# Cross-attention probabilities turned by VectorE and DMA in place of TensorE, the division moved behind the weighting

## What is computed

```python
q_big = einsum('bshk,hkq->bshq', (x @ Wq.T).reshape(8, 56, 16, 128), w_kc_q)   # 16 heads
kv_r = rope(kv_c)                                  # context, 8 x 1500 x 64
q_r = einsum('bshq,hqr->bhsr', rope(q_big), W_qr)  # layer 3: no rope on q
k_r = einsum('bld,hdr->bhlr', kv_r, W_kr)
scores = einsum('bhsr,bhlr->bhsl', q_r, k_r)
attn = softmax(scores, axis=-1)                    # over the 1500 context rows
ctx_c = einsum('bhsl,bld->bhsd', attn, kv_r)       # the weighted context
out = einsum('bhsd,hkd->bhsk', ctx_c, w_kc_kv) @ Wo.T
```

## Time and profile before

| | |
|---|---|
| time, median of 3 runs | 1666.74 us (1664.62 to 1668.67) |
| profiled execution, its span | 1666.3 us |
| PE busy | 1627.4 us, 98% |
| PEld busy | 1104.8 us, 66% |
| DVE busy | 1113.9 us, 67% |
| ACT busy | 749.9 us, 45% |
| POOL busy | 239.1 us, 14% |
| DMA | 71.10 MB, mean 43 GB/s |

### The profile page before, as it was taken

How to read it: one execution, slowest core, us unless ns; L and a number is a source line. 1 busy time by engine, 2 the same in 40 slices (tenths; PEclk the granted TensorE clock), 3 DMA queues, 4 the chain that set the end, 5 groups by cost and what they waited for, 6 DMA issues and landing times.

```text
span 1666.3 us, 35653 instructions
## 1 busy us (share of the span) xinstructions
PE 1627.4 (98%) x15234; PEld 1104.8 (66%) x15234; DVE 1113.9 (67%) x1974; ACT 749.9 (45%) x1297; POOL 239.1 (14%) x428
## 2 busy tenths in 40 slices
PE   9999999999999899999999999999999999999998
PEld 5575367777755666655377777764566767777765
DVE  3735899999566763266899999435445289999623
ACT  2223366666413641144366666312444366666411
POOL 0011300000010313011200000010455000000030
PEclk9999999999999999999999999999999999999999
DMA  8302020000040011051020000050300220000010
GB/s 280 86 13 83 1 78 2 2 2 2 2 187 1 2 59 40 1 133 48 1 97 2 2 2 2 4 240 0 64 1 1 114 89 2 2 2 2 2 44 11
DMA packets 35522, 71.10 MB, mean 43 GB/s; under 512 B 25359, under 2 KB 29775, under 8 KB 31433
## 3 DMA queue, kind: packets, MB, share of 16 engines
q1 hardware_dynamic: 35240, 68.71, 12.6%
q10 hardware_dynamic: 126, 0.11, 0.0%
HBM read 68.36 MB, written 0.46 MB: 41 GB/s over the span
## 4 chain that ended last, share of the span: by engine, by line
PE 89%; DVE 6%; ACT 2%; POOL 1%; issue 1%; DMA 1%; SPq 0%; DVEq 0%; POOLq 0%; ACTq 0%
PE ps L1122 14%; PE ps L1135 14%; PE ps L1035 13%; PE ps L1501 9%; PE ps L361 9%; PE ps L946 3%; PE ps L2599 3%; PE ps L1150 3%; PE ps L528 2%; PE ps L1961 2%; PE ps L956 1%; POOL arena L1795 1%; PE ps L2626 1%; PE ps L982 1%; PE ps L967 1%
## 5 line engine op out<-in xcount | busy, mean ns | idle before, releaser
L1236 ACT ACTIVATE arena<-ps,softmax_stats 128x1500 f32<-128x1500 f32 x168 | 253.8, 1511 | 193.0 <-DVE softmax_stats L1317 190.8
L1135 PEld LDWEIGHTS ps<-arena,ctx_pos 125*64 125x64 f32 x4608 | 222.3, 137 | 58.4 <-issue 55.4
L1122 PE MATMUL ps<-ident,arena 64*125 64x64 f32 x4032 | 239.1, 271 | 1.9 <-ACT arena L1236 1.6
L1135 PE MATMUL ps<-arena,ctx_pos 125*64 125x128 f32 (+1 forms) x4608 | 240.5, 262 | 0.0
L1122 PEld LDWEIGHTS ps<-ident,arena 64*125 64x125 f32 x4032 | 226.8, 185 | 17.0 <-issue 13.5
L1035 PE MATMUL ps<-ctx_feat,arena 64*128 64x500 f32 x1008 | 230.5, 590 | 0.0
L1243 ACT COPY arena<-ps 125x512 f32<-125x512 f32 x336 | 172.5, 600 | 77.9 <-PE ps L1122 77.9
L1315 DVE TENSOR_REDUCE softmax_stats<-ps 128x1 f32<-128x500 f32 x252 | 170.6, 678 | 49.0 <-PE ps L1035 48.6
L361 PE MATMUL ps<-arena 128*128 128x256 f32 x736 | 174.7, 383 | 3.5 <-DVE arena L1630 1.2
L1328 DVE TENSOR_SCALAR arena<-arena,softmax_stats 128x1500 f32<-128x1500 f32 x168 | 168.3, 1002 | 5.9
L1501 PE MATMUL ps<-x_feat,arena 128*128 128x448 f32 (+1 forms) x416 | 167.9, 549 | 1.2 <-DVE arena L1613 1.2
(11 more groups left out here) (324 smaller groups left out, 1931.7 us busy)
## 6 DMA issues: line engine op xcount, KB each, us to landing
ctx_pos<-in_ctx SPq DMA_DIRECT2D x1, 2688.0 KB
arena<-in_L1f_gate SPq DMA_DIRECT2D x1, 2304.0 KB, 12.1
arena<-in_L1f_up SPq DMA_DIRECT2D x1, 2304.0 KB, 17.0
arena<-in_L1f_down SPq DMA_DIRECT2D x1, 2304.0 KB, 7.8
arena<-in_L0a_Wq SPq DMA_DIRECT2D x1, 2048.0 KB, 10.9
arena<-in_L0a_Wc SPq DMA_DIRECT2D x1, 2048.0 KB, 18.8
arena<-in_L0x_Wq SPq DMA_DIRECT2D x1, 2048.0 KB, 9.9
arena<-in_L0x_Wo SPq DMA_DIRECT2D x1, 2048.0 KB, 8.3
```

The costliest lines, as they stand in the source:

```text
L1122: m = nc.tensor.transpose(c.ps[0:LP, turn_bank(i, k, r), n * 64:(n + 1) * 64], probs[i % 2][e][rows, l * LP:(l + 1) * LP], c.ident[rows, r ...
L1135: m = nc.tensor.matmul(y[r * 64:(r + 1) * 64, lo:hi], c.ctx_pos[:, j, l, e, :], pT[i % 2][:, lo // 64:hi // 64, LT * e + l, :], start=(l = ...
L1236: nc.scalar.activation(probs[i % 2][e].rearrange("p (k l) -> p k l", k=3), sc[e], ACT.Exp, bias=low[:, i % 4, e:e + 1], accum_out=total[:, ...
```

## The change

Of the 24 blocks of probabilities of a unit (12 tiles for each e) TensorE turns only 6: tiles 0 to 5 of e = 1 (`BY_PE`). The other 18 are turned by VectorE in blocks of 32 x 32 (`turn_blocks`), straight from the undivided exponentials, which now stand 128 apart (`LQ`) instead of 125. A 32 x 32 transpose leaves each block in its own quarter of the partitions. So 16 DMAs a unit, one for each pair of quarters, move 32 rows of 576 numbers (`RUN`) from `blocks` to `moved_to`. SP issues them when both transposes of a unit are done.

The probabilities are no longer divided. Instead the reciprocals are laid on a diagonal by GpSimd (`spread_out`), spread over 64 partitions by a matmul with ones (`spread`), copied to `rinv` by ScalarE (`keep_spread`), and multiplied into the weighted context by GpSimd when it is placed (`place_context`; for the last unit VectorE, `keep_last`). `keep` goes from VectorE to ScalarE. `prefetch` goes from SP to ScalarE's queue.

```diff
+LQ, BY_PE = 32 * 4, 6
+RUN = 32 * (2 * LT - BY_PE)
...
     @block.sync
...
-        sp.wait_ge(lat_in.handle, lat_in.at(4 * NH // 2))
-        prefetch(sp)
+        for i in range(NU):
+            sp.wait_ge(blocked[1].handle, blocked[1].at(i + 1))
+            if i >= 2:
+                sp.wait_ge(pv_mm.handle, pv_mm.at(i - 1))
+            for frm in range(4):
+                for to in range(4):
+                    sp.dma_start(moved_to[i % 2][32 * to:32 * to + 32, frm, :],
+                                 blocks[i % 2][32 * frm:32 * frm + 32, to, :]).then_inc(moved[i % 2].handle, 16)
+                    moved[i % 2].n += 16
...
     @block.gpsimd
+        def spread_out(i):
+            pool.wait_ge(recip.handle, recip.at(i + 1))
...
+            for e in range(2):
+                nc.gpsimd.tensor_scalar(diag[i % 2][:, e, :], c.ident[:], inv[:, i % 4, e:e + 1], 1.0, ALU.mult, ALU.mult).then_inc(*diag_in.next())
+
+        def place_context(i):
...
+                nc.gpsimd.tensor_tensor(ctxT[rows, 2 * j + e, at + lo:at + hi], held[i % 2][rows, lo:hi],
+                                        rinv[i % 2][rows, lo:hi], ALU.mult).then_inc(*ct_in.next())
...
     @block.tensor
+        def turn(i):
+
+            pe.wait_ge(exped[1].handle, exped[1].at(i + 1))
...
+                pe.wait_ge(b_in.handle, b_in.at(2 * i))
+                pe.wait_ge(rinv_in.handle, rinv_in.at(i))
+            for l in range(BY_PE):
                 for r in range(2):
...
+        def spread(i):
+
+            pe.wait_ge(diag_in.handle, diag_in.at(2 * i + 2))
+            for r, e, lo, hi in parts(i % UNITS):
+                m = nc.tensor.matmul(spread_ps[r * 64:(r + 1) * 64, lo:hi], ones, diag[i % 2][:, e, lo:hi], start=True, stop=True,
+                                     skip_group_check=True)
+            m.then_inc(*spread_mm.next())
...
         def weigh(i):
...
-            pe.wait_ge(a_in.handle, a_in.at(4 * (i + 1)))
-            pe.wait_ge(d_in.handle, d_in.at(2 * (i + 1)))
+            pe.wait_ge(b_in.handle, b_in.at(2 * (i + 1)))
+            pe.wait_ge(moved[i % 2].handle, moved[i % 2].at(256 * (i // 2 + 1)))
+            if i > 0:
+                pe.wait_ge(kept.handle, kept.at(i))
...
+                    if e == 1 and l < BY_PE:
+                        p = pT[i % 2][:, lo // 64:hi // 64, l, :]
+                    else:
+                        at = 32 * (LT * e + l - BY_PE * e)
+                        p = moved_to[i % 2][0:LP, lo // 32:hi // 32, at:at + 32]
...
     @block.scalar
+        for i in range(NU + 2):
+            if i >= 3:
+                keep(i - 3)
+            if i >= 2:
+                copy_turned(i - 2, 0)
+                copy_turned(i - 2, 1)
+                keep_spread(i - 2)
             if i < NU:
                 exp(i, 0)
                 exp(i, 1)
             if i == 0:
                 cm_out(3)
                 place(7)
...
+                act.wait_ge(lat_in.handle, lat_in.at(4 * NH // 2))
+                prefetch(act)
...
     @block.vector
+        def turn_blocks(i, e):
             dve.wait_ge(exped[e].handle, exped[e].at(i + 1))
...
+            if i >= 2 and e == 0:
+                dve.wait_ge(moved[i % 2].handle, moved[i % 2].at(256 * (i // 2)))
+            n = BY_PE * e
+            nc.vector.transpose(blocks[i % 2][:, :, 32 * LT * e:32 * (LT + (LT - n) * e)].rearrange("p g (l h) -> p g l h", h=32),
+                                probs[i % 2][e][:, n * LQ:].rearrange("p (l g q) -> p g l q", g=4, q=32)).then_inc(*blocked[e].next())
...
+        for i in range(NU):
+            rowmax(i)
+            if i == 0:
+                cm_out(2)
+            turn_blocks(i, 0)
+            turn_blocks(i, 1)
+            invert(i)
```

More of the change, by code:

```diff
@@ L901, in _ @@
                     nc.gpsimd.tensor_tensor(rot2[p % 2][:, n], cos2[:, n], sin2[:, n], ALU.add).then_inc(*rot2_in.next())
+        pool.wait_ge(cm_mm.handle, cm_mm.at(4))
+        nc.gpsimd.memset(ones, 1.0).then_inc(*padded.next())
         pool.wait_ge(padded.handle, padded.last())
-        for i in range(NU - 1):
+        def spread_out(i):
+            pool.wait_ge(recip.handle, recip.at(i + 1))
+            if i >= 4:
+                pool.wait_ge(ct_in.handle, ct_in.last())
+            if i >= 2:
+                pool.wait_ge(spread_mm.handle, spread_mm.at(i - 1))
+            for e in range(2):
+                nc.gpsimd.tensor_scalar(diag[i % 2][:, e, :], c.ident[:], inv[:, i % 4, e:e + 1], 1.0, ALU.mult, ALU.mult).then_inc(*diag_in.next())
+        def place_context(i):
             j, u = i // UNITS, i % UNITS
+            pool.wait_ge(diag_in.handle, diag_in.last())
+            pool.wait_ge(rinv_in.handle, rinv_in.at(i + 1))
             pool.wait_ge(kept.handle, kept.at(i + 1))
@@ L1027, in score @@
                     pe.wait_ge(exped[e].handle, exped[e].at(i))
[L1028 to L1031, removed]
             j, u = i // UNITS, i % UNITS
@@ L1121, in turn @@
                     rows = slice(r * 64, (r + 1) * 64)
-                    m = nc.tensor.transpose(c.ps[0:LP, turn_bank(i, k, r), n * 64:(n + 1) * 64],
-                                            probs[i % 2][e][rows, l * LP:(l + 1) * LP], c.ident[rows, rows])
-                    if n == 7:
+                    m = nc.tensor.transpose(turn_place(r)[:, l * 64:(l + 1) * 64],
+                                            probs[i % 2][1][rows, l * LQ:l * LQ + LP], c.ident[rows, rows])
+                    if l == BY_PE - 1:
@@ L1164, in _ @@
                 weigh(i - 2)
-            for k in turn_order(i - 1):
-                turn(i - 1, k)
-        pe.wait_ge(d_in.handle, d_in.at(2 * (NU - 1)))
+            turn(i - 1)
+            spread(i - 1)
         project(0)
@@ L1170, in _ @@
         project(1)
-        for k in range(3):
-            turn(NU - 1, k)
+        turn(NU - 1)
+        spread(NU - 1)
         project(2)
```

125 lines of the change are left out of this document (54 added, 71 removed).

## The result

The changed kernel takes 1886.18 us (median of 4 runs, 1874.71 to 1890.55) against 1667.7 us for the kernel before on the same chip: a ratio of 1.129 (95% interval 1.124 to 1.134). It is 13% slower where I forecast 2.6% faster, and it lies far beyond the range. The profiled execution spans 1872.9 us.

What follows compares the result with a forecast made beforehand. SP's 16 issues a unit (7.6 us) were to pace the kernel above the loop's 7.0: a stage of 8.0 + 205.2 + 2.2 + 13.7 = 229.1 us against 245.7, less 2 us at the start, 44 saved over three stages, 1623 us, range 1575 to 1703.

Steps and rivals of the forecast that it cites:

- I take 0.47, the row nearest in form: SP's queue: 16 issues a unit at 0.47 us plus 0.1 for the wait, 7.6 us; chance 0.47.
- the row of 0.42 us: SP's queue before the change: a 32-row issue read as standing alone, 0.42 us, the next starting 0.47 after it.
- the slower rival: SP's queue: issues beyond 0.51 us lose the gain; 1703 us at 0.53, 1745 at 8.99 a burst; chance 0.22.
- the formula: Cross-attention stage: with a unit period P it takes 23.9 + 27 P us, breaking even near P = 8.2.
- issues hidden: SP's queue: issues of 0.43 us or less, so the score-maxima-exponential loop sets 7.0 us a unit, 1575 us; chance 0.18.
- VectorE: VectorE's round in a unit: transposes 2.71 us and maxima 4.18, together 6.89 us, not above the loop's 7.0.
- the rival at 2.88 and 1.44: VectorE's transposes run like L1300: 8.5 us a round, 1695 us; chance 0.07.
- TensorE: TensorE's work in a unit: scoring 2.67, weighting 2.77, turning 0.67, spreading 0.23, together 6.34 us, under the 7.0.
- The landing: Weighting's wait for moved pieces: they land 2.2 us after issue.
- The start: Stage start: unit 0's blocks ready at 8.0 us, plus 2 us for loads moved to ScalarE's queue, bounds 0 and 6.
- The clock: TensorE: 3.4 us a unit at half clock loses 1.7 us, giving 8.0 us a unit, 1655 us; chance 0.06.
- The rule weighed against the row: SP's issues: by the skill's rule only the bytes count, 2.9 us, giving 7.0 for 7.6; the trace's 0.47 was preferred.

Runs made afterwards that it cites:

- the last kernel: Changed kernel with 9 transfers on SP, 3 on ScalarE, 4 GpSimd copies; ScalarE issues before its reciprocal copy, GpSimd places context before its copies: 1608.06 us, ratio 0.963.
- the kernel of 1927 us: Changed kernel with 9 transfers on SP, 3 on ScalarE behind its reciprocal copy, 4 GpSimd copies ahead of placing the context: 1927.49 us, ratio 1.155.

## Why the prediction was wrong

**The bound was right.** It said that SP's issues pace the unit, and it named the likeliest way to miss. Issues stand back to back, weighting waits for pieces, and the time doesn't answer to half the bytes but to half the issues.

**The step that failed is "I take 0.47, the row nearest in form": the term 16 x 0.47 + 0.1 = 7.6 us a unit.** It measured 16 x 0.671 = 10.7 us, and by the first and last issue of the three stages (302.9, 301.3 and 302.1 us for 447 intervals) 10.8. Two things are in it. The row was near in partitions, but it read HBM; the run from HBM shows that 32 rows of 2304 bytes cost 0.464 us from there and 0.633 from SBUF: 16 x 0.17 = 2.7 us. And issues stall now and then, which a row of one issue can't show: 16 x (0.676 - 0.633) = 0.7 us here.

Nor did the row of 0.42 us stand alone, as the prediction read it. It is the last of nine issues back to back in the trace of the kernel before:

```profile
72.43 5.04 SPq L125 DMA_DIRECT2D arena<-in_q_rope  x9
```

Four of the nine have 32 rows in one piece each and took 0.62, 0.42, 0.58 and 0.42 us; the mean of the nine, 0.56, gives the 9.1 us a unit and the 1745 us of the slower rival. The bursts of 16 in the earlier trace rows, 0.62 and 0.56 each, hold stalls too: three issues of the first and one of the second took 0.95 to 1.39 us, and most others 0.47. I set them aside for having more pieces, but they read HBM as well. No row of the kernel before shows a DMA from SBUF to SBUF, so none held the right price: even the bound of 10.0 us a unit, which the prediction named and left out of its range, gives 1817 us, and 10.8 lies beyond it. The prediction's own sensitivity, 13 us for 0.01 us an issue, asked for a wider range than 1575 to 1703.

With 10.8 the formula gives 23.9 + 27 x 10.8 = 315.5 a stage; less 245.7, times three, with the start's 6 us: 1666.7 + 215 = 1882 us, against 1886 measured. The stages of the profiled execution bear it out: from the first scores to the end of the last weighting they take 319.3, 316.5 and 317.4 us, where the formula with the start's 2 us gives 317.5. The rest of that execution is 10 us shorter than before, which the sum doesn't have and no run explains, and its runs spread over 16 us; that the total comes within 4 us of the median is partly luck.

**The rival "the issues are slower"** was the case that came, given 0.22 and priced up to 1745 us, 141 us too little.

**The rival "issues hidden"** named the right floor: its loop of 7.0 us is the 7.07 of the last kernel. That kernel's 1608 us isn't 1575, since not every unit of a stage keeps to it: from SP's first issue to its last the three stages take 203.7, 208.9 and 207.1 us, 7.3 to 7.5 a unit, and 27 units at 0.4 us more, three times, are about the 33 us between. What makes those units longer is not taken apart further.

**VectorE** was right. Groups by shape in the steady stretch of the changed kernel (busy, mean ns, idle before):

```profile
L1382 DVE STREAM_TRANSPOSE arena<-arena 128x1536 f32<-128x1536 f32 x18 | 32.0, 1778 | 10.8 <-DMA arena<-arena 10.3
...
L1382 DVE STREAM_TRANSPOSE arena<-arena 128x768 f32<-128x768 f32 x17 | 15.9, 936 | 0.0
```

1.778 and 0.936 us against 1.758 and 0.950 in the sum: the row of equal length was the right one, and the rival at 2.88 and 1.44 is out. The second 768 elements cost 842 ns, 1.10 ns each. The Trainium skill (Vector Engine (DVE) Microarchitecture Reference, The reshape front-end and per-opcode configuration) has the transpose sustain one element per cycle per lane; this trace is in line with it as far as it shows: maxima over 500 and 1500 elements (0.68 and 1.71 us) differ by 1.03 ns an element, nearly the same pace, but how long a cycle is, no run here shows.

**TensorE** was a little low: from start to start turning and spreading take 0.80 and 0.38 us (251.68, 252.48, 252.86), not 0.67 and 0.23, which nothing shows in the time. **The landing** (2.2 forecast) is 2.1.

**The start** came out at the forecast size for another reason. SP's first piece starts at 212.5, 10.2 us after the first scores (202.35), where 8.0 + 2 were forecast. But ScalarE issues the moved loads from 211.72 to 214.32, and its next exponential starts at 214.50, 0.03 us after the maximum that it needs: the loads delay nothing there. What is late is VectorE's first transpose, at 209.85. It waits for other matmuls of TensorE (L969) that end at 209.72, while its exponential was done at 207.76. The match with 8.0 + 2 is luck.

**The clock** fell about as its rival said: 0.86 over the stretch, where 3.4 us of 8.0 at half clock would be 0.79, and a weighting of 4.51 us has lost the 1.7 us that it named. But the rival let TensorE pace the unit at 8.0 us; under SP's 10.8 the loss costs nothing in the steady stretch, since SP waited for a weighting only once.

**The rule weighed against the row.** The Trainium skill (DMA: Bandwidth & Descriptors, Issuing engines are not separate DMA queues) calls the time to start a DMA usually small relative to the DMA. For one DMA that holds here: an issue is 0.59 us beside 2.1 us to landing. But 16 issues stand in series on one queue, and so the term that the rule lets one leave out is the bound: halving the bytes changed nothing and halving the issues gave 283 us. The measurement decides.

## What to carry to other kernels

A DMA has a price on the queue that issues it, here the same for 1152 and 2304 bytes a row and for 32 and 64 rows: count the issues of a unit, take the price from a burst of the same kind (same source, back to back, stalls included), and compare it with the unit's shortest loop before any byte. If it is near, cut the number of issues or share them between queues, since another queue's issues come at nearly the same price beside it (615 and 591 ns). But place what you share out behind no wait and ahead of nothing urgent: the same work on the same engines took 1927 or 1608 us by the order of two lines.

## What was not expected of the hardware

- A 32-row issue on SP has an interval of 0.633 us when it reads SBUF and 0.464 when it reads HBM. It is the same for 1152 and 2304 bytes a row (591 ns), and nearly so for 32 and 64 rows (591 and 597).
- ScalarE's queue asks about the same (median 615 ns), and SP's issues stay at 592 while ScalarE issues.
- In each stage 18 to 21 of SP's 448 issues take 0.3 to 1.6 us longer than the median, with full bytes, half bytes and from HBM alike, though a stage's issues take 302, 298 and 233 us. SP's own count doesn't set their number: 224 issues of 64 rows have 12 to 15 a stage, and SP's 252 have 9 to 11 in the kernel of 1927 us and 15 to 19 in that of 1608. Next to the stall at 258.44 one packet of the queue for instructions falls in the window, 258.4 to 260.4:

```profile
q1 hardware_dynamic: 94, 0.15, 31.2%
q8 instruction: 1, 0.02, 4.2%
```

That is no accident. Counted in the changed kernel's trace, 55 of the 59 long issues end within 2.0 us of the start of a packet of that queue, which 3.5% of the ordinary issues do, and 55 of the 56 packets of the three stages are followed by a long issue. The packets go with TensorE's matmuls. The whole spans of the kernel before, the changed one and the one with idle matmuls have:

```profile
q8 instruction: 121, 1.98, 0.5%
...
q8 instruction: 100, 1.64, 0.4%
...
q8 instruction: 108, 1.77, 0.4%
```

TensorE has 15234, 12594 and 13530 matmuls there, 125 or 126 to a packet in each. With the idle matmuls a stage has 22 packets in place of 18 or 19, and 21 to 25 long issues. So SP's issues stall beside the loading of TensorE's instructions, as far as counts and times show it; how the one holds up the other stays open. So does what in an SBUF source costs the 0.17 us.

- GpSimd's copy of 32 x 576 takes 0.659 us, where I had estimated 1.1 between two of its other rows.
